# Recurrent LSTM and RNN on one core: ScalarE's bias copy and GpSimd's sums of x are issued at other places

## The chip, the cores and the metric

The kernel runs on one core of one Trainium2 chip. The metric is the device time of one execution in microseconds (us); the number compared is the median of several executions. Times of single instructions come from one further execution, taken with the hardware profiler.

## The reference

Two recurrent layers run one after the other over 512 steps, with 16 sequences side by side and 512 features. Each layer's output is added to its input.

```
# layer 0, an LSTM (xW = x @ Wx + b, h starts at cond_1024, c at 0)
a = xw_t + prev_h @ Wh                      # 16 x 2048
i, f, o = sigmoid(a[:, :H]), sigmoid(a[:, H:2H]), sigmoid(a[:, 2H:3H]);  g = tanh(a[:, 3H:])
next_c = f * prev_c + i * g
next_h = o * tanh(next_c)
x = x + all the next_h
# layer 1, a plain RNN on the new x (h starts at cond_1024)
h_next = tanh(h @ Wh + xw_t)                # 16 x 512
x = x + all the h_next
```

## The kernel before

Everything is transposed: features lie on the 128 partitions, and 512 features are four slices of 128 (`SUB`). TensorE works with four column groups of 32 (`QUADS`), so a "matmul" of the trace is one of four that run beside each other in the array (`128*32` in the rows). The state h is held as an fp16 high part and an fp16 low part, side by side as 32 columns. The recurrent weights of the LSTM are also split in two fp16 tiles.

**One pass of the loop is one step t of the LSTM and, beside it, step s = t - 4 (ScalarE, TensorE) of the RNN.** There is no scheduler: each engine has its own list of instructions, written by hand, in order, and semaphores tie the lists together. In the trace's names, in the order in which TensorE takes them in step t:

- `rec_first_ps` and `rec_second_ps`: 32 matmuls each, the two halves of `prev_h @ Wh`. The first half begins when the low part of the first half of h is ready (`h0_ready[0]`, VectorE line 536), and its second 16 matmuls wait for `h0_ready[1]`, the same line for the second half of h.
- "units", on `in_ps` and `c_ps`: the products x @ Wx of later steps, in fp32. Four steps (a span) need 14 units of 8 matmuls, and they are dealt out as 4, 3, 4, 3 over steps with (t + 5) % 4 = 0, 1, 2, 3. So odd steps have 32 such matmuls and even steps 24. They use sums and differences of blocks of x (`x_sums`), which is how seven products do the work of eight.
- `rnn_ps<-wx_sb,y`: the RNN's x @ Wx for two of its steps at once (`input1`), 24 matmuls in an even step and 8 in an odd one.
- `rnn_ps<-wh_parts,h_parts`: 16 matmuls, the RNN's recurrent product (`recurrent1`).

Before `input1`, TensorE waits for the RNN's seed of this step (`seed1_done`), and in odd steps also for `in1_biased`: ScalarE has then written the bias b1 for the RNN's steps s + 3 and s + 4 into one of two places of `rnn_ps` (`bias1`, line 652). That place has just been read by `seed1(s)` (line 680), which is why the copy can't come before it.

VectorE turns the products (line 483, `turned<-rec_first_ps` and `rec_second_ps`), adds the two parts of h (line 489), forms the cell and then h (lines 509, 514, 524, 529, 536), and writes x + h (line 544, `y<-h_full,x_sb`). In between it handles the RNN: line 550 (`rec_sum<-rnn_ps,rec_low`), the turn at line 556, the add at line 561 (`pre<-turned`), lines 566 and 571 for the RNN's new state. ScalarE writes seeds into PSUM (lines 669, 680) and takes the tanh of the gates (line 693), of the RNN (688) and of the cell (703).

GpSimd, after its setup, does only the sums of x. In each chunk of 16 steps it makes four instructions (line 211, `x_sums`), one per step, for the next chunk, whose units begin at step 11 of the current one. All their operands are in SBUF. The table is `if 3 <= c < 7` at line 235, and each is released by `rec0_done[0]`, the end of the step's `rec_first_ps` matmuls.

Of the kernel before, what the change touches and what calls it, by code (L numbers as in the profile page):

```python
# [19 lines left out]
CHUNKS = STEPS // CHUNK  # L20
# [3 lines left out]
PAIRS = STEPS // PAIR  # L24
SPAN = 2 * PAIR
SPANS, PER_CHUNK = STEPS // SPAN, CHUNK // SPAN
UNITS_OF_PART = (0, 4, 7, 11, 14)
SLOTS = SPAN * SPANS - 5
Y0_PAIRS = 4
LAG = 4  # L30
H_SCALE = 2.0 ** 15
# [8 lines left out]
def residual_lstm_rnn(nc, xT, h0T, wx0, wh0, b0, wx1, wh1, b1, yT):  # L40
    with ExitStack() as ctx:
# [86 lines left out]
        rec0_done, turned0_done, pre0_done = (sem_by_half(n) for n in ("rec0_done", "turned0_done", "pre0_done"))  # L128
        gates_done, uv_done, cell_done = (sem_by_half(n) for n in ("gates_done", "uv_done", "cell_done"))
        o_scaled_done, tanh_c_done = sem_by_half("o_scaled_done"), sem_by_half("tanh_c_done")  # L130
        h0_full_done, h0_ready = sem_by_half("h0_full_done"), sem_by_half("h0_ready")
        y0_done = sem("y0_done")

        in1_biased, in1_done, seed1_done = sem("in1_biased"), sem("in1_done"), sem("seed1_done")
# [52 lines left out]
        @block.gpsimd  # L187
        def _(pool):
            nc.gpsimd.memset(zeros[:, :], 0.0).then_inc(zeroed, 1)
            nc.gpsimd.memset(h_first[:, :, :], 0.0).then_inc(h_zeroed, 1)  # L190
            nc.gpsimd.memset(gates_cell[:, :, GATES], 0.0).then_inc(cell_zeroed, 1)
            nc.gpsimd.iota(partition[:, :], [[0, 1]], 0, 1).then_inc(numbered, 1)
            def reduce_largest(l):
                pool.wait_ge(largest_done, l + 1)
                nc.gpsimd.partition_all_reduce(largest_all[l][:, :], largest[l][:, :], P,
                                               bass.bass_isa.ReduceOp.max).then_inc(reduced, 1)

            def sum_x(v, i):

                x = x_sb[:, v % 2].rearrange("p k (g r t) n -> p r k g (t n)", g=PER_CHUNK, r=2)  # L200
                a11, a12, a21, a22 = x[:, 0, 0:SUBH], x[:, 0, SUBH:SUB], x[:, 1, 0:SUBH], x[:, 1, SUBH:SUB]
                sums = x_sums[:, v % 2]
                if i == 0:
                    pool.wait_ge(x_in[v % 2], loads(v))
                    if v >= 2:
                        pool.wait_ge(slot_done, slots_until((v - 1) * CHUNK - 6))
                if i in (1, 3):
                    pool.wait_ge(x_summed, 4 * v + i)
                out, one, op, other = ((sums[:, 0], a21, ALU.add, a22), (sums[:, 1], sums[:, 0], ALU.subtract, a11),
                                       (sums[:, 2], a11, ALU.subtract, a21), (sums[:, 3], a12, ALU.subtract, sums[:, 1]))[i]  # L210
                nc.gpsimd.tensor_tensor(out, one, other, op).then_inc(x_summed, 1)  # L211

            def sum_wx0(i):

                b11, b12 = wx0_sb[:, 0:SUBH, :, 0:COLSH], wx0_sb[:, 0:SUBH, :, COLSH:COLS]
                b21, b22 = wx0_sb[:, SUBH:SUB, :, 0:COLSH], wx0_sb[:, SUBH:SUB, :, COLSH:COLS]
                if i < 2:
                    pool.wait_ge(wx0_doubled, SUBH * (i + 1))
                if i in (1, 3):
                    pool.wait_ge(wx0_summed, i)  # L220
                one, other = ((b12, b11), (b22, wx0_sums[:, 0]), (b22, b12), (b21, wx0_sums[:, 1]))[i]
                nc.gpsimd.tensor_tensor(wx0_sums[:, i], one, other, ALU.subtract).then_inc(wx0_summed, 1)

            pool.wait_ge(b0_doubled, 1)
            nc.gpsimd.tensor_tensor(b0_diff[:, :], b0_sb[:, COLSH:COLS], b0_sb[:, 0:COLSH], ALU.subtract).then_inc(b0_diff_done, 1)
            for i in range(4):
                sum_x(0, i)
            reduce_largest(0)
            for i in range(4):
                sum_wx0(i)  # L230

            reduce_largest(1)
            for t in range(STEPS):
                v, c = divmod(t, CHUNK)
                if 3 <= c < 7 and v + 1 < CHUNKS:
                    pool.wait_ge(rec0_done[0], t + 1)
                    sum_x(v + 1, c - 3)

        @block.tensor
        def _(pe):  # L240
# [391 lines left out]
        def _(act):  # L632
# [18 lines left out]
            def bias1(r):  # L651
                nc.scalar.activation(in1_ps[r % 2], b1_sb[:, :], ACT.Copy).then_inc(in1_biased, 1)
# [21 lines left out]
            def seed1(s):  # L674

                act.wait_ge(in1_done, s // PAIR + 1)
                if s:
                    act.wait_ge(rec1_summed, s)
                own = (mask_scaled[1] if s else mask_half)[:, s % PAIR:s % PAIR + 1]
                nc.scalar.activation(rec1_by_part, in1_by_part(s // PAIR % 2), ACT.Copy, scale=own).then_inc(seed1_done, 1)  # L680
# [58 lines left out]
            for t in range(END):  # L739
                s = t - LAG  # L740
                g, part = divmod(t + 5, SPAN)
                ahead = t < SLOTS
                if t < STEPS:
                    act.wait_ge(slot_done, slots_until(t - 1))
                    if t:
                        seed0(1, t)
                if s >= 1:
                    copy_low1(s - 1)
                if t < STEPS:
                    if t + 1 < STEPS:  # L750
                        seed0(0, t + 1)
                    if t == 1:
                        copy_v(1)
                    if part == 0 and g < SPANS:
                        act.wait_ge(seed0_done[0], t + 2)
                        bias_z(g).then_inc(z_biased, 1)
                    elif part == 1 and ahead:
                        act.wait_ge(seed0_done[0], t + 2)
                        if g > 1:
                            copy_v(g)  # L760
                        begin_c11(g).then_inc(c11_begun, 1)
                    elif part == 3 and g + 1 < SPANS:
                        bias_v(g + 1).then_inc(v_biased, 1)
                if t == 3:
                    act.wait_ge(scaled, 2)
                    for k in range(SUB):
                        high_part(wh1_sb[:, k].rearrange("p q (b c) -> p (q b) c", c=QUAD), 1,
                                  wh1_parts[:, k, :, :, 0].rearrange("p q b c -> p (q b) c"))
                if 0 <= s < STEPS:
                    seed1(s)  # L770
                if t < STEPS:
                    gates(0, t)
                if s >= 1:
                    tanh1(s - 1)
                if t < STEPS:
                    o_half(0, t)
                    gates(1, t)
                    tanh_cell(0, t)
                if s >= 0 and s % 2 and s // 2 + 2 < PAIRS:

                    act.wait_ge(seed1_done, s + 1)
                    bias1(s // 2 + 2)
                if t < STEPS:
                    o_half(1, t)
                    tanh_cell(1, t)
# [39 lines left out]
```

## Time and profile before

| | us |
|---|---|
| three timed executions, median | 2277.07 |
| lowest and highest | 2273.94 and 2279.57 |
| the profiled execution | 2289.59 |
| its span, first to last instruction | 2287.8 |
| PE busy | 2210.8 (97%) |
| VectorE (DVE) busy | 2100.8 (92%) |
| ScalarE (ACT) busy | 1782.7 (78%) |
| GpSimd (POOL) busy | 116.1 (5%) |

The span lies 1.8 us inside its execution, and that execution is 12.5 us longer than the median of the timed ones. The granted TensorE clock was 0.987 on the mean. The 512 steps fill nearly the whole span, in a steady rhythm: a step takes some 4.3 us. TensorE's matmuls overlap and their ends are modelled, so "busy" does not mean that the array has work all the time; what the engine does between two groups is better seen from the starts of the groups.

### The profile page before, as it was taken

The page shows a single profiled execution, that of the slowest core. Times are in us where ns is not written, and L with a number is a line of the kernel's source. Part 1 is how long each engine was busy: PE and PEld are TensorE (multiplying, and loading weights), DVE is VectorE, ACT ScalarE, POOL GpSimd, SP SyncE. Part 2 cuts the span into 40 slices and gives each one's busy share as a digit, 9 for nine tenths or more (in the row PEclk, how much of TensorE's full clock was granted, in tenths as well). Part 3 has the DMA queues.
Part 4 walks back from the last instruction along what each step waited for, and adds up shares of the span by engine and source line. Part 5 has one row for each costly group of instructions (what it writes and reads, how often), then busy time and mean ns, then how long its engine had stood idle before and what let it go on. Part 6 is the DMA issues. An engine that isn't in the chain of part 4 may idle for free.

```text
span 2287.8 us, 148190 instructions
## 1 busy us (share of the span) xinstructions
PE 2210.8 (97%) x63548; PEld 1835.4 (80%) x63548; DVE 2100.8 (92%) x11050; ACT 1782.7 (78%) x6431; POOL 116.1 (5%) x143
## 2 busy tenths in 40 slices
PE   3899999999999999999999999999999999999996
PEld 1688888888888888888888888888888888888885
DVE  6899999999999999999998999899999999899997
ACT  3688787887887788777887788778887888778885
POOL 4000000000000000000000000000000000000000
PEclk7999999999999999999999999999999999999998
DMA  5000000000000000000000000000000000000000
GB/s 209 3 23 23 18 23 14 18 22 23 18 23 13 18 23 22 18 16 19 18 23 21 19 13 23 18 23 18 23 13 18 23 23 18 22 14 18 23 13 12
DMA packets 16733, 53.88 MB, mean 24 GB/s; under 512 B 2256, under 2 KB 2384, under 8 KB 14800
## 3 DMA queue, kind: packets, MB, share of 16 engines
q1 hardware_dynamic: 16080, 44.41, 5.4%
q8 instruction: 503, 8.24, 1.5%
q14 instruction: 150, 1.23, 0.2%
HBM read 27.62 MB, written 16.78 MB: 19 GB/s over the span
## 4 chain that ended last, share of the span: by engine, by line
PE 95%; DVE 2%; issue 1%; ACT 1%; DMA 1%; POOL 0%; SPq 0%; DVEq 0%; ACTq 0%; POOLq 0%
PE in_ps L244 24%; PE rnn_ps L244 22%; PE rec_first_ps L244 20%; PE rec_second_ps L244 19%; PE c_ps L244 10%; DVE wh_part L452 1%; DMA x_sb<-xT 1%; ACT wh_part L658 0%; DVE turned L483 0%; DVE wh_parts L452 0%; POOL x_sums L211 0%; ACT wh_parts L658 0%; DVE largest_slice L407 0%; ACT gates_cell L693 0%; DVE pre_sb L489 0%
## 5 line engine op out<-in xcount | busy, mean ns | idle before, releaser
L244 PE MATMUL rec_first_ps<-wh_part,h_parts 128*32 128x256 f16 x16352 | 561.2, 273 | 20.7 <-DVE h_parts L536 20.6
L244 PE MATMUL rec_second_ps<-wh_part,h_parts 128*32 128x256 f16 x16352 | 560.9, 273 | 0.1
L244 PEld LDWEIGHTS rec_first_ps<-wh_part,h_parts 128*32 128x32 f16 x16352 | 436.3, 96 | 59.5 <-issue 32.2
L244 PEld LDWEIGHTS rec_second_ps<-wh_part,h_parts 128*32 128x32 f16 x16352 | 469.0, 97 | 1.1 <-issue 0.3
L244 PE MATMUL in_ps<-wx_sums,x_sums 128*32 128x256 f32 x6096 | 417.3, 379 | 2.2 <-issue 1.2
L244 PEld LDWEIGHTS rnn_ps<-wx_sb,y 128*32 128x32 f32 x8192 | 249.7, 109 | 156.4 <-issue 126.8
L693 ACT ACTIVATE gates_cell<-gate_ps,unscale 128x128 f32<-128x128 f32 x511 | 187.9, 368 | 240.3 <-DVE gate_ps L489 237.9
L244 PE MATMUL rnn_ps<-wx_sb,y 128*32 128x128 f32 x8192 | 347.6, 275 | 13.0 <-issue 6.3
L244 PE MATMUL rnn_ps<-wh_parts,h_parts 128*32 128x256 f16 x8176 | 344.8, 274 | 8.2 <-DVE h_parts L571 8.2
L244 PEld LDWEIGHTS in_ps<-wx_sums,x_sums 128*32 128x32 f32 x6096 | 225.2, 110 | 92.7 <-issue 4.7
L244 PEld LDWEIGHTS rnn_ps<-wh_parts,h_parts 128*32 128x32 f16 x8176 | 249.9, 97 | 11.4 <-issue 8.5
L483 DVE STREAM_TRANSPOSE turned<-rec_second_ps 128x256 f32<-128x256 f32 x512 | 228.9, 447 | 18.8 <-PE rec_second_ps L244 0.9
L550 DVE TENSOR_TENSOR rec_sum<-rnn_ps,rec_low 128x128 f32<-128x128 f32 x512 | 149.5, 292 | 94.7 <-ACT rec_low L684 88.6
L680 ACT ACTIVATE rnn_ps<-rnn_ps,mask_scaled 128x256 f32<-128x256 f32 x511 | 225.4, 441 | 12.7 <-DVE rec_sum L550 2.5
L693 ACT ACTIVATE gates_cell<-pre_sb,unscale 128x128 f32<-128x128 f32 x511 | 205.4, 402 | 30.6 <-DVE pre_sb L489 1.3
L509 DVE SCALAR_TENSOR_TENSOR uv<-gates_cell 128x64 f32<-128x64 f32 x1024 | 227.2, 222 | 1.8 <-ACT gates_cell L693 1.4
L684 ACT ACTIVATE rec_low<-rnn_ps 128x128 f32<-128x128 f32 x512 | 142.1, 278 | 107.9 <-PE rnn_ps L244 96.1
L483 DVE STREAM_TRANSPOSE turned<-rec_first_ps 128x256 f32<-128x256 f32 x512 | 219.9, 430 | 2.5 <-PE rec_first_ps L244 1.1
L698 ACT ACTIVATE o_scaled<-gates_cell 128x32 f32<-128x32 f32 x1024 | 219.8, 215 | 0.2
L536 DVE TENSOR_TENSOR h_parts<-h_full,h_parts 128x32 f16<-128x32 f32 x1024 | 193.0, 188 | 17.9
L244 PE MATMUL c_ps<-wx_sb,x_sb 128*32 128x256 f32 x2096 | 174.6, 383 | 24.1 <-ACT wx_sb L634 24.0
L514 DVE SCALAR_TENSOR_TENSOR gates_cell<-uv 128x32 f32<-128x32 f32 x1024 | 193.6, 189 | 0.2
(93 smaller groups left out, 3575.8 us busy)
## 6 DMA issues: line engine op xcount, KB each, us to landing
x_sb<-xT SPq DMA_DIRECT2D x32, 512.0 KB, 4.1
yT<-y SPq DMA_DIRECT2D x64, 256.0 KB, 2.4
wh_sb<-wh SPq DMA_DIRECT2D x5, 1024.0 KB, 9.0
wx_sb<-wx SPq DMA_DIRECT2D x5, 1024.0 KB, 14.4
b_sb<-b SPq DMA_DIRECT2D x1, 256.0 KB, 2.7
b_sb<-b SPq DMA_DIRECT2D x1, 64.0 KB, 11.6
h_first<-h0T SPq DMA_DIRECT2D x1, 32.0 KB, 11.3
```

Source lines behind the costliest of these rows:

```text
L244: last = nc.tensor.matmul(out[QUAD * q:QUAD * (q + 1)], states, weights(q), start=False, stop=True, tile_position=(0, QUAD * q), skip_grou ...
L452: return nc.vector.scalar_tensor_tensor(low, w32, w_scale[l][:, :], high, ALU.mult, ALU.subtract)
L483: nc.vector.transpose(turned0[:, half].rearrange("p b n -> p (b n)"), rec0_ps(t, half)).then_inc(turned0_done[half], 1)
L509: nc.vector.scalar_tensor_tensor(uv[:, half], gates_cell[:, half, 0:2], 1.0, gates_cell[:, half, 3:5], ALU.add, ALU.mult).then_inc(uv_done ...
L514: nc.vector.scalar_tensor_tensor(gates_cell[:, half, GATES], uv[:, half, 1], 0.5, uv[:, half, 0], ALU.mult, ALU.add).then_inc(cell_done[ha ...
L536: nc.vector.tensor_tensor(h0_parts[:, subs, BATCH:], slices(h0_full[:, cols]), h0_parts[:, subs, 0:BATCH], ALU.subtract).then_inc(h0_ready ...
L550: nc.vector.tensor_tensor(rec1_sum[:, :, :], rec1_by_part[:, :, 0], rec1_low[:, :, :], ALU.add).then_inc(rec1_summed, 1)
L680: nc.scalar.activation(rec1_by_part, in1_by_part(s // PAIR % 2), ACT.Copy, scale=own).then_inc(seed1_done, 1)
L684: nc.scalar.activation(rec1_low[:, :, :], rec1_by_part[:, :, 1], ACT.Copy).then_inc(rec1_copied, 1)
L693: nc.scalar.activation(gates_cell[:, half, 0:GATES].rearrange("p g n -> p (g n)"), pre0[half], ACT.Tanh, scale=unscale[0][:, :] if t else ...
L698: nc.scalar.activation(o_scaled[:, half], gates_cell[:, half, 2], ACT.Copy, bias=H_SCALE / 2, scale=H_SCALE / 2).then_inc(o_scaled_done[ha ...
```

## The change

Two moves; no instruction is added or removed.

1. ScalarE: `bias1` of odd RNN steps is issued straight behind `seed1`, ahead of the tanh of the first half's gates. Before it stood behind `tanh_cell(0, t)`. It still waits for `seed1_done`.
2. GpSimd: the four sums of a chunk are made in steps 3, 4, 7 and 8 instead of 3, 4, 5 and 6, and each waits for `h0_ready[1]` to reach t (the state that step t starts from is complete) instead of `rec0_done[0]` reaching t + 1 (step t's first product is done).

```diff
+STEPS_OF_X_SUMS = (3, 4, 7, 8)
...
             for t in range(STEPS):
                 v, c = divmod(t, CHUNK)
-                if 3 <= c < 7 and v + 1 < CHUNKS:
-                    pool.wait_ge(rec0_done[0], t + 1)
-                    sum_x(v + 1, c - 3)
+                if c in STEPS_OF_X_SUMS and v + 1 < CHUNKS:
+                    pool.wait_ge(h0_ready[1], t)
+                    sum_x(v + 1, STEPS_OF_X_SUMS.index(c))
...
                 if 0 <= s < STEPS:
                     seed1(s)
+                if s >= 0 and s % 2 and s // 2 + 2 < PAIRS:
+
+                    act.wait_ge(seed1_done, s + 1)
+                    bias1(s // 2 + 2)
                 if t < STEPS:
                     gates(0, t)
                 if s >= 1:
...
                     gates(1, t)
                     tanh_cell(0, t)
-                if s >= 0 and s % 2 and s // 2 + 2 < PAIRS:
-
-                    act.wait_ge(seed1_done, s + 1)
-                    bias1(s // 2 + 2)
                 if t < STEPS:
                     o_half(1, t)
                     tanh_cell(1, t)
```

ScalarE's list in an odd step (t = 7), before, from the second half's seed to the last tanh. `rnn_ps<-b_sb` is the bias copy, `rnn_ps<-rnn_ps,mask_scaled` the RNN's seed:

```order
L669 ACTIVATE rec_second_ps<-c_sb,mask_scaled 128x256 [waits turned0_done_1,slot_done]
L684 ACTIVATE rec_low<-rnn_ps 128x128 [waits rec1_done]
L669 ACTIVATE rec_first_ps<-c_ps,mask_scaled 128x256 [waits turned0_done_0]
L637 ACTIVATE in_ps<-b_sb 128x256 [waits seed0_done_0]
L680 ACTIVATE rnn_ps<-rnn_ps,mask_scaled 128x256 [waits rec1_summed,in1_done]
L693 ACTIVATE gates_cell<-gate_ps,unscale 128x128 [waits pre0_done_0]
L688 ACTIVATE h_full<-pre,unscale 128x64 [waits pre1_done]
L698 ACTIVATE o_scaled<-gates_cell 128x32 [waits gates_done_0]
L693 ACTIVATE gates_cell<-pre_sb,unscale 128x128 [waits pre0_done_1]
L703 ACTIVATE gate_ps<-gates_cell 128x32 [waits cell_done_0]
L652 ACTIVATE rnn_ps<-b_sb 128x128 [waits seed1_done]
L698 ACTIVATE o_scaled<-gates_cell 128x32 [waits gates_done_1]
```

The same place in the changed kernel, whose lines are numbered one higher:

```order
L670 ACTIVATE rec_second_ps<-c_sb,mask_scaled 128x256 [waits turned0_done_1,slot_done]
L685 ACTIVATE rec_low<-rnn_ps 128x128 [waits rec1_done]
L670 ACTIVATE rec_first_ps<-c_ps,mask_scaled 128x256 [waits turned0_done_0]
L638 ACTIVATE in_ps<-b_sb 128x256 [waits seed0_done_0]
L681 ACTIVATE rnn_ps<-rnn_ps,mask_scaled 128x256 [waits rec1_summed,in1_done]
L653 ACTIVATE rnn_ps<-b_sb 128x128 [waits seed1_done]
L694 ACTIVATE gates_cell<-gate_ps,unscale 128x128 [waits pre0_done_0]
L689 ACTIVATE h_full<-pre,unscale 128x64 [waits pre1_done]
L699 ACTIVATE o_scaled<-gates_cell 128x32 [waits gates_done_0]
L694 ACTIVATE gates_cell<-pre_sb,unscale 128x128 [waits pre0_done_1]
L704 ACTIVATE gate_ps<-gates_cell 128x32 [waits cell_done_0]
L699 ACTIVATE o_scaled<-gates_cell 128x32 [waits gates_done_1]
```

The bias copy moved five places forward: it now stands in front of the tanh of the first gates, directly behind the instruction whose semaphore it waits for.

GpSimd's list of the first sums in the loop, before (the four of chunk 1 and the first of chunk 2):

```order
L211 TENSOR_TENSOR x_sums<-x_sb 128x256 [waits x_in1,rec0_done_0]
L211 TENSOR_TENSOR x_sums<-x_sums,x_sb 128x256 [waits x_summed,rec0_done_0]
L211 TENSOR_TENSOR x_sums<-x_sb 128x256 [waits rec0_done_0]
L211 TENSOR_TENSOR x_sums<-x_sb,x_sums 128x256 [waits x_summed,rec0_done_0]
L211 TENSOR_TENSOR x_sums<-x_sb 128x256 [waits slot_done,x_in0,rec0_done_0]
```

And in the changed kernel:

```order
L212 TENSOR_TENSOR x_sums<-x_sb 128x256 [waits x_in1,h0_ready_1]
L212 TENSOR_TENSOR x_sums<-x_sums,x_sb 128x256 [waits x_summed,h0_ready_1]
L212 TENSOR_TENSOR x_sums<-x_sb 128x256 [waits h0_ready_1]
L212 TENSOR_TENSOR x_sums<-x_sb,x_sums 128x256 [waits x_summed,h0_ready_1]
L212 TENSOR_TENSOR x_sums<-x_sb 128x256 [waits slot_done,x_in0,h0_ready_1]
```

Their order is the same; what releases each of them is another semaphore (and, for the third and fourth, a later step).

## Rows read from the trace of the kernel before

**Rows 1.** The page: busy us of each engine, share of the span, count.

```profile
PE 2210.8 (97%) x63548; PEld 1835.4 (80%) x63548; DVE 2100.8 (92%) x11050; ACT 1782.7 (78%) x6431; POOL 116.1 (5%) x143
```

**Rows 2.** Waits: engine, releaser, us in total, times, longest us.

```profile
PEld rnn_ps L244 <- issue: 135.3, 277, 2.7
...
PE rec_first_ps L244 <- DVE h_parts L536: 20.6, 7, 16.0
```

**Rows 3.** Timeline of odd step 203: start us, length us, engine, operation, count.

```profile
937.24 1.05 PE L244 MATMUL in_ps<-wx_sb,x_sb 128*32 128x256 f32 x16
...
938.78 0.26 ACT L652 ACTIVATE rnn_ps<-b_sb 128x128 f32<-128x128 f32 x1
...
939.11 0.19 PEld L244 LDWEIGHTS rnn_ps<-wx_sb,y 128*32 128x32 f32 x8 [0.44 <-issue]
...
939.14 0.43 PE L244 MATMUL rnn_ps<-wx_sb,y 128*32 128x128 f32 x8
...
939.30 0.19 DVE L536 TENSOR_TENSOR h_parts<-h_full,h_parts 128x32 f16<-128x32 f32 x1
...
939.36 0.65 PE L244 MATMUL rnn_ps<-wh_parts,h_parts 128*32 128x256 f16 x16
...
939.80 1.08 PE L244 MATMUL rec_first_ps<-wh_part,h_parts 128*32 128x256 f16 x32
```

**Rows 4.** Timeline of even step 204, matmuls (PE), weight loads (PEld), VectorE.

```profile
941.54 1.07 PE L244 MATMUL in_ps<-wx_sums,x_sums 128*32 128x256 f32 x16
...
942.84 0.87 PE L244 MATMUL rnn_ps<-wx_sb,y 128*32 128x128 f32 x24
...
943.62 0.19 DVE L536 TENSOR_TENSOR h_parts<-h_full,h_parts 128x32 f16<-128x32 f32 x1
...
943.93 0.81 PEld L244 LDWEIGHTS rec_first_ps<-wh_part,h_parts 128*32 128x32 f16 x32
...
943.96 1.06 PE L244 MATMUL rec_first_ps<-wh_part,h_parts 128*32 128x256 f16 x32
```

**Rows 5.** Timeline of ScalarE in odd step 203.

```profile
936.69 0.43 ACT L680 ACTIVATE rnn_ps<-rnn_ps,mask_scaled 128x256 f32<-128x256 f32 x1
...
937.42 0.37 ACT L693 ACTIVATE gates_cell<-gate_ps,unscale 128x128 f32<-128x128 f32 x1 [0.30 <-DVE gate_ps L489]
...
938.28 0.40 ACT L693 ACTIVATE gates_cell<-pre_sb,unscale 128x128 f32<-128x128 f32 x1
```

**Rows 6.** Timeline around one sum of x (POOL) and VectorE beside it.

```profile
1050.08 0.30 DVE L556 STREAM_TRANSPOSE turned<-rec_sum 128x128 f32<-128x128 f32 x1
1050.27 0.73 POOL L211 TENSOR_TENSOR x_sums<-x_sb 128x256 f32<-128x256 f32 x1 [3.51 <-PE rec_first_ps L244]
1050.31 0.41 DVE L483 STREAM_TRANSPOSE turned<-rec_first_ps 128x256 f32<-128x256 f32 x1
1050.64 0.44 DVE L561 TENSOR_TENSOR pre<-turned 128x64 f32<-128x64 f32 x1
```

**Rows 7.** Line 561: length ns min/median/max, first and last start.

```profile
L561 DVE TENSOR_TENSOR pre<-turned x512: 179/184/492, 85.9 to 2284.1; 128x64 f32<-128x64 f32 x171
```

**Rows 8.** Line 211, in the same columns.

```profile
L211 POOL TENSOR_TENSOR x_sums<-x_sums,x_sb x32: 729/733/1247, 15.8 to 2151.3; 128x256 f32<-128x256 f32 x32
```

**Rows 9.** Stretches of four steps: length, busy us (count) by engine, clock, DMA.

```profile
902.35:919.67 17.32, 17.15 (x506) 14.07 (x497) 16.48 (x88) 13.69 (x52) 2.93 (x4) 1.00 0.06 19
936.60:953.53 16.93, 16.93 (x505) 14.07 (x497) 15.88 (x87) 13.80 (x51) 0.00 (x0) 1.00 0.06 20
```

**Rows 10.** Timeline of VectorE from the end of step 203 into step 204.

```profile
939.81 0.18 DVE L536 TENSOR_TENSOR h_parts<-h_full,h_parts 128x32 f16<-128x32 f32 x1
...
939.91 0.22 DVE L544 SCALAR_TENSOR_TENSOR y<-h_full,x_sb 128x64 f32<-128x64 f32 x1
...
940.36 0.29 DVE L550 TENSOR_TENSOR rec_sum<-rnn_ps,rec_low 128x128 f32<-128x128 f32 x1 [0.23 <-ACT rec_low L684]
...
941.29 0.18 DVE L561 TENSOR_TENSOR pre<-turned 128x64 f32<-128x64 f32 x1
```

## The prediction

> **What bounds the kernel now.** I read the page's first part, then the view of waits, then two steps instruction by instruction, then GpSimd's four instructions of a chunk.
>
> The page has TensorE busy for 97% of the span, VectorE for 92% [rows 1]. That could mean a kernel bound by matmuls, where nothing that ScalarE or GpSimd does can matter. The view of waits says otherwise: TensorE's weight loads for the RNN stood still 277 times, 135.3 us in all, 0.49 us each [rows 2]. The releaser is given as "issue", so the profile doesn't name it. But 277 is little more than 254, the number of odd RNN steps with a bias copy (s = 1, 3, ..., 507), and the timeline shows it. In odd step 203 the units begin at 937.24, the bias copy runs from 938.78 to 939.04, and the weight loads of `input1` begin at 939.11 after 0.44 us of idle time, 0.07 us behind the copy's end; the first matmul is at 939.14 [rows 3]. So TensorE waits for the copy in every odd step.
>
> Those 0.44 us are not what the wait costs, because loads run ahead of matmuls. The cost is read from the starts of the matmuls. In even step 204, 24 fp32 matmuls of the units lie between 941.54 and 942.84: 1.30 us, 0.054 us each [rows 4]. Thirty-two take 1.73 us, so in step 203 `input1` could begin at 937.24 + 1.73 = 938.97 and not at 939.14. The wait costs 0.17 us of a step.
>
> The second bound is the state. In step 204 the first half's low part ends at 943.62 + 0.19 = 943.81, the weight loads of the next `rec_first_ps` begin 0.12 us later, at 943.93, and its matmuls at 943.96 [rows 4]. That is a wait for the state, which only just binds: from the end of line 536 to the first matmul there are 0.15 us. In step 203 the same part ends at 939.49, and the matmuls begin at 939.80, 0.31 us later [rows 3]: there the state is early and TensorE late. From one `rec_first_ps` to the next, step 204 takes 943.96 - 939.80 = 4.16 us, with the state as its limit.
>
> **Part one, the bias copy.** Nothing is added, one copy of 0.26 us moves. On ScalarE the RNN's seed ends at 937.12 and the tanh of the first gates begins at 937.42, when VectorE has its input [rows 5]. The copy waits for the seed's own semaphore, for which I take 0.03 us: 937.15 to 937.41. It fits into the hole of 0.30 us with 0.01 us to spare. If it is late by some hundredths, the tanh of the first gates is late by as much; that tanh has no hurry, because ScalarE's next one that matters starts at 938.28 for an input of its own. In its old place the copy ran while VectorE formed the second cell, so its leaving speeds up nothing on ScalarE.
>
> TensorE then finds the copy done 1.5 us before it asks. `input1` starts at 938.97. The RNN's product starts 0.22 us later (939.36 - 939.14) and the next `rec_first_ps` 0.44 us after that (939.80 - 939.36) [rows 3]: 939.63. What is late next is the state: 939.49 + 0.15 = 939.64. The two limits nearly meet, and the gain is 939.80 - 939.64 = 0.16 us. I take 0.15, as one step's difference is read to 0.01 and the other kind of odd step may have less. 254 x 0.15 = 38.1 us. Bounds: TensorE can't gain more than the 0.17 of the wait, 43 us; it gains nothing if the state, once pulled, comes no earlier. The state should follow, since everything between two states starts from TensorE's products. I take off 2 us for odd steps in which TensorE's stalls of other kinds are now hidden in the wait (23 of the 277 are such, if all 254 are the copy's): 36 us.
>
> **Part two, the sums.** A sum takes 0.73 us on GpSimd, and it is always followed by the same thing. The one at 1050.27 ends at 1051.00. VectorE's add of line 561, with both inputs in SBUF, begins at 1050.64 and takes 0.44 us; it ends at 1051.08, 0.08 us behind the sum. The transpose before it (one input, in PSUM) ran from 1050.31 for 0.41 us, inside the sum, and the transpose at 1050.08 (one input, in SBUF) overlaps it as well; neither kept the other up [rows 6]. Line 561 has a median of 184 ns and a maximum of 492 [rows 7], so the sums hold it up by up to 0.3 us. It also goes the other way: one sum took 1247 ns where 733 is the median [rows 8], at 79.2 us, among VectorE's long two-input instructions of the setup. One waits for the whole of the other.
>
> The Trainium skill ("SBUF — State Buffer", § Who interferes with whom) states that a VectorE instruction with two SBUF inputs and a GpSimd instruction that reads SBUF share one port pair, that whichever starts first keeps it for its whole length, and that VectorE with at most one SBUF input doesn't contend. The rows agree so far.
>
> The price comes from two stretches that begin and end at the same place of the rhythm: four steps with four sums take 17.32 us, four without any 16.93 [rows 9]. So a chunk's sums cost 0.39 us, and 31 chunks 12.1 us.
>
> Where do they fall in the changed kernel? The state is complete at 939.81 + 0.18 = 939.99. The y add of line 544 is then already running, 939.91 to 940.13, and has two SBUF inputs. Line 550 at 940.36 has one input in PSUM, and line 561 comes at 941.29 [rows 10], some 0.16 us earlier in the new rhythm: 941.13. A sum released at 939.99 runs from about 940.03, or from 940.13 if it has to let the y add finish, and ends at 940.76 to 940.86. Nothing with two SBUF inputs is due until 941.13. The sums become free: 12 us are saved. The same stretch ahead of the other kind of chosen step is shorter but, by the same count, holds a sum too. The fourth sum is ready in step 8 and needed in step 11, so no unit is late, and no queue stands behind GpSimd's wait, as it has no other work.
>
> **The sum.** 36 + 12 = 48 us, from the profiled execution's 2289.6 to 2241.6 (span 2287.8 to 2240). The timed median is 12.5 us below the profiled execution; taking the same 48 from it gives 2229. I say 2230.
>
> **Rivals.**
>
> A. *The state doesn't follow.* The new limit of an odd step lies 0.01 us from TensorE's own, and every chain through ScalarE and VectorE is close. If an odd step gains 0.05 instead of 0.15, part one brings 12.7 us, and the whole 25: 2252. For it speaks that VectorE is busy for 92%; against it that the state of step 203 waits 0.16 us unused today.
>
> B. *The sum overtakes the y add.* The sum is released at 939.99, 0.08 us after the add's row begins [rows 10]. If the add doesn't hold the port by then, it waits for the sum, as line 561 does, and ends at 940.03 + 0.73 + 0.08 = 940.84. Line 550 is queued behind it and would start near 940.8, not at 940.36 - 0.16 = 940.20: 0.6 us late. Part of that is slack: the second turn waits for `rec_second_ps` anyway, and I put this slack at 0.2 us. 0.4 x 124 sums = 50 us, which eats all 48: 2279, no change. The 1247 ns sum speaks against it, for there the instruction that was running went first.
>
> C. *The same mechanism at full price*, with no slack in the turn: 0.6 x 124 = 74 us against 48, slower by 26 us: 2303. It ends on the slower side once a sum costs over (48 + 7) / 124 = 0.44 us. The place is the two-input add ahead of line 550, and the price is the 0.6 above.
>
> By the Trainium skill's rule of who starts first (same page and section) the y add, whose row begins 0.08 us ahead of the release, keeps the port, and B and C don't happen; no row shows two such instructions that close.
>
> D. *The bias copy isn't what TensorE waits for* but `seed1_done` or y. Then only the sums' 12 us remain: 2265. The 0.07 us between the copy's end and the loads speaks against it.
>
> **How the numbers follow.** The forecast has 0.68, A 0.14, B 0.06, C 0.04, D 0.04, and 0.04 goes to something not seen, spread evenly over both signs. A measurement of this kernel can't tell less than about 0.3% (7 us) from no change. A and D are faster by more than that. Faster: 0.68 + 0.14 + 0.04 + 0.02 = 0.88. Same: B with a bit of the rest, 0.07. Slower: 0.05. The range begins where the whole wait of 0.17 is won and 0.39 per chunk too (55 us: 2222), with 4 us for what a single profile misses, and reaches past A: 2218 to 2256.
>
> **What the new profile would show.** The 277 waits of the weight loads for `rnn_ps` fall to some tens. In an odd step the matmuls of `input1` begin 1.73 us behind the first of the units, and `rec_first_ps` 0.15 us behind the end of line 536 in every step, odd or even. The bias copy sits between the RNN's seed and the first gates' tanh, which hardly moves. Line 561 has no length above 0.2 us in the loop, and line 544 stays at 0.22; B and C would show it at 0.8 or more. Sums have 0.73 to 0.85 us. Four steps take 16.93 - 2 x 0.15 = 16.63 us with sums and without. The prediction is wrong if the four steps stay near 16.9, or if those with sums are longer than those without.

## The result: 2214.9 us, 2.8% faster, and more than predicted

The changed kernel takes 2214.85 us in the median of four executions (2212.09 to 2216.77), the kernel before 2278.32 beside it. The ratio is 0.9724, with a 95% interval of 0.9706 to 0.9741: faster by 63 us, where 48 were predicted. The time lies 3 us below the low end of the range (2218). The direction and both mechanisms held; the size was too small.

The profiled execution is one of the four, 2214.99 us, with a span of 2213.2. Its first part answers to [rows 1]:

```profile
PE 2146.7 (97%) x63548; PEld 1769.1 (80%) x63548; DVE 2092.3 (95%) x11050; ACT 1808.4 (82%) x6431; POOL 116.5 (5%) x143
```

The same 97% of TensorE, in a kernel that is 3% shorter: this share says nothing about the wait that went. The view of waits (engine, what was waited for, us in total, times, longest) does, where [rows 2] had 135.3 us in 277 waits for `rnn_ps`:

```profile
PEld rec_first_ps L245 <- issue: 25.6, 21, 16.5
PE rec_first_ps L245 <- DVE h_parts L537: 20.6, 8, 16.0
...
PEld rnn_ps L245 <- issue: 8.0, 3, 2.7
```

Three waits are left of 277. In the timeline of odd step 203, which answers to [rows 3] and [rows 5] (start and length in us):

```profile
911.04 0.43 ACT L681 ACTIVATE rnn_ps<-rnn_ps,mask_scaled 128x256 f32<-128x256 f32 x1
...
911.50 0.28 ACT L653 ACTIVATE rnn_ps<-b_sb 128x128 f32<-128x128 f32 x1
911.59 1.05 PE L245 MATMUL in_ps<-wx_sb,x_sb 128*32 128x256 f32 x16
911.77 0.37 ACT L694 ACTIVATE gates_cell<-gate_ps,unscale 128x128 f32<-128x128 f32 x1
...
913.32 0.41 PE L245 MATMUL rnn_ps<-wx_sb,y 128*32 128x128 f32 x8
...
913.65 0.19 DVE L537 TENSOR_TENSOR h_parts<-h_full,h_parts 128x32 f16<-128x32 f32 x1
...
913.99 1.06 PE L245 MATMUL rec_first_ps<-wh_part,h_parts 128*32 128x256 f16 x32
```

The copy follows its seed, and the first gates' tanh still begins 0.73 us behind that seed's start (937.42 - 936.69 before, 911.77 - 911.04 now). The RNN's input product begins 913.32 - 911.59 = 1.73 us behind the units, as computed. The next `rec_first_ps` begins 0.15 us behind the end of line 537 (913.65 + 0.19 = 913.84): the state's limit. Even step 204 answers to [rows 4]:

```profile
917.80 0.19 DVE L537 TENSOR_TENSOR h_parts<-h_full,h_parts 128x32 f16<-128x32 f32 x1
918.11 0.81 PEld L245 LDWEIGHTS rec_first_ps<-wh_part,h_parts 128*32 128x32 f16 x32
918.14 1.06 PE L245 MATMUL rec_first_ps<-wh_part,h_parts 128*32 128x256 f16 x32
```

From 913.99 to 918.14 are 4.15 us, with 0.15 us behind line 537 again. It is so throughout: in 99% of the steps from 30 to 490 of this trace that distance is 0.15 us, where the kernel before has it at the end of undisturbed even steps alone (42% of all steps; 0.30 us in a typical odd one). The state is now the limit of odd and even steps alike.

A sum of x and VectorE beside it, from the timeline at step 200:

```profile
897.58 0.18 DVE L537 TENSOR_TENSOR h_parts<-h_full,h_parts 128x32 f16<-128x32 f32 x1
897.68 0.22 DVE L545 SCALAR_TENSOR_TENSOR y<-h_full,x_sb 128x64 f32<-128x64 f32 x1
897.84 0.73 POOL L212 TENSOR_TENSOR x_sums<-x_sb,x_sums 128x256 f32<-128x256 f32 x1 [3.42 <-DVE h_parts L537]
897.92 0.29 DVE L551 TENSOR_TENSOR rec_sum<-rnn_ps,rec_low 128x128 f32<-128x128 f32 x1
...
898.88 0.18 DVE L562 TENSOR_TENSOR pre<-turned 128x64 f32<-128x64 f32 x1
```

The sum starts 0.08 us behind the complete state and ends at 898.57. The y add keeps its 0.22 us, line 551 its 0.29 beside the sum, and line 562, the add that used to wait, starts 0.31 us after the sum's end. Over the whole kernel (length in ns: min/median/max) line 562 answers to [rows 7], whose maximum was 492; the y add of line 545, beside which each of the 120 sums of the 480 steps from 16 to 496 starts, never took more than 222:

```profile
L562 DVE TENSOR_TENSOR pre<-turned x512: 182/183/226, 87.4 to 2209.5; 128x64 f32<-128x64 f32 x171
L545 DVE SCALAR_TENSOR_TENSOR y<-h_full,x_sb x512: 216/219/222, 64.0 to 2195.1; 128x64 f32<-128x64 f32 x171
```

### The profile page after: what moved, and what is told of

Same layout as the page of the kernel before. It is cut to its first block, busy times and chain, and to the rows that moved or that the text cites. A ratio compares the mean times of both kernels' runs of the same rounds, so it can differ in the third digit from the quotient of the medians.

```text
span 2213.2 us, 148190 instructions
## 1 busy us (share of the span) xinstructions
PE 2146.7 (97%) x63548; PEld 1769.1 (80%) x63548; DVE 2092.3 (95%) x11050; ACT 1808.4 (82%) x6431; POOL 116.5 (5%) x143
## 4 chain that ended last, share of the span: by engine, by line
PE 95%; DVE 2%; issue 1%; ACT 1%; DMA 1%; POOL 0%; SPq 0%; DVEq 0%; ACTq 0%; POOLq 0%
PE in_ps L245 25%; PE rec_first_ps L245 21%; PE rec_second_ps L245 20%; PE rnn_ps L245 20%; PE c_ps L245 10%; DVE wh_part L453 1%; DMA x_sb<-xT 1%; ACT wh_part L659 0%; DVE turned L484 0%; DVE wh_parts L453 0%; POOL x_sums L212 0%; DVE uv L510 0%; ACT wh_parts L659 0%; DVE largest_slice L408 0%; DVE pre_sb L490 0%
## 5 line engine op out<-in xcount | busy, mean ns | idle before, releaser
L245 PE MATMUL rec_first_ps<-wh_part,h_parts 128*32 128x256 f16 x16352 | 545.4, 274 | 20.9 <-DVE h_parts L537 20.6
L245 PE MATMUL rec_second_ps<-wh_part,h_parts 128*32 128x256 f16 x16352 | 544.5, 273 | 0.0
L245 PEld LDWEIGHTS rec_first_ps<-wh_part,h_parts 128*32 128x32 f16 x16352 | 377.8, 95 | 105.9 <-issue 25.3
L245 PEld LDWEIGHTS rec_second_ps<-wh_part,h_parts 128*32 128x32 f16 x16352 | 454.3, 97 | 0.4
L245 PE MATMUL in_ps<-wx_sums,x_sums 128*32 128x256 f32 x6096 | 402.1, 379 | 1.4 <-ACT rec_first_ps L670 0.7
L245 PE MATMUL rnn_ps<-wh_parts,h_parts 128*32 128x256 f16 x8176 | 322.0, 273 | 11.7 <-DVE h_parts L572 11.7
L245 PE MATMUL rnn_ps<-wx_sb,y 128*32 128x128 f32 x8192 | 321.9, 273 | 1.5 <-ACT rnn_ps L681 1.5
L245 PEld LDWEIGHTS in_ps<-wx_sums,x_sums 128*32 128x32 f32 x6096 | 206.0, 110 | 102.2 <-issue 2.1
L245 PEld LDWEIGHTS rnn_ps<-wh_parts,h_parts 128*32 128x32 f16 x8176 | 230.6, 97 | 14.6 <-issue 8.0
L704 ACT ACTIVATE tanh_c_sb<-gates_cell 128x32 f32<-128x32 f32 x512 | 118.0, 231 | 108.5 <-DVE gates_cell L515 108.5
```

The source lines that it names most:

```text
L245: last = nc.tensor.matmul(out[QUAD * q:QUAD * (q + 1)], states, weights(q), start=False, stop=True, tile_position=(0, QUAD * q), skip_grou ...
L704: nc.scalar.activation(tanh_c[half], gates_cell[:, half, GATES], ACT.Tanh, scale=0.5).then_inc(tanh_c_done[half], 1)
```

## The experiments

All are timed against the kernel before, on the same chip in the same job; its medians there were 2278.7 to 2282.4. The changed kernel's 2214.9 comes from a job of its own (2278.3 before), so differences of some 4 us from it are within what the jobs differ by. Two numbers are read from each profile. Steps 16 to 496 are cut into 30 chunks of 16 steps, each from the start of one step's turn of `rec_first_ps` (line 484 in the changed kernel, 483 in the one before) to that of the step 16 later. The **regular time** is the shortest of these chunks, which holds four sums like every other. The **irregular time** is what the 480 steps take beyond 30 times the regular time.

### Each part alone

The copy moved, the sums as before:

```diff
-                if c in STEPS_OF_X_SUMS and v + 1 < CHUNKS:
-                    pool.wait_ge(h0_ready[1], t)
-                    sum_x(v + 1, STEPS_OF_X_SUMS.index(c))
+                if 3 <= c < 7 and v + 1 < CHUNKS:
+                    pool.wait_ge(rec0_done[0], t + 1)
+                    sum_x(v + 1, c - 3)
```

> The bias copy moved as in the change; the sums of x as in the kernel before. Theory 1 (two separate parts: the copy's place is worth 0.165 us in each of 254 odd steps, 42 us, and with it most of TensorE's irregular stalls go, some 9 us): 51 us below before, 2227. Theory 2 (the stalls go with the sums, not with the copy): 42 us below, 2236. Theory 3 (the sums' contention costs more once the state bounds every step, since all of it lands on the state): less than 40 us, 2240 or more.

Measured: 2223.39 us, ratio 0.9749 (0.9725 to 0.9772), 56 us below before.

The sums moved, the copy as before (the change's second part alone):

```diff
-                if 3 <= c < 7 and v + 1 < CHUNKS:
-                    pool.wait_ge(rec0_done[0], t + 1)
+                if c in STEPS_OF_X_SUMS and v + 1 < CHUNKS:
+                    pool.wait_ge(h0_ready[1], t)
```

> The sums of x as in the changed kernel; the bias copy in its old place. Theory 1: 12 us below before, 2266, and the stalls are still there. Theory 2: 12 + 9 = 21 us below, 2257. Theory 3: under 12 us.

Measured: 2265.04 us, ratio 0.9933 (0.9909 to 0.9956), 14.5 us below before. With the changed kernel at 2214.9, the sums' move is worth 8.5 us when the copy has been moved. Theory 1 comes closest, with 51 and 12 us expected for the two parts alone and 56 and 14.5 measured. Theory 2 (42 us and 21) and theory 3 fall.

### Does anything remain?

The changed kernel with sums for two chunks only:

```diff
-                if c in STEPS_OF_X_SUMS and v + 1 < CHUNKS:
+                if c in STEPS_OF_X_SUMS and v + 1 < 2:
...
-                pe.wait_ge(x_summed, 4 * (g // PER_CHUNK) + i + 1)
+                pe.wait_ge(x_summed, min(4 * (g // PER_CHUNK) + i + 1, 8))
```

> The changed kernel with the sums of x made only for the first two chunks; all later chunks use those. If the sums are free in their new place, as the prediction says, the time is the changed kernel's, 2215 within 3 us. If they still hold something up, it is lower by what they cost.

Measured: 2212.17 us. Its regular time is 66.32 us against 66.37: by that, 120 sums together cost under 2 us; by the timed medians the kernel is 2.7 us faster. The sums are as good as free.

The kernel before without the loop's bias copies and TensorE's waits for them:

```diff
-                if s >= 0 and s % 2 and s // 2 + 2 < PAIRS:
-
-                    act.wait_ge(seed1_done, s + 1)
-                    bias1(s // 2 + 2)
...
-                    if s % 2 and s // 2 + 2 < PAIRS:
-                        pe.wait_ge(in1_biased, s // 2 + 3)
...
-                pe.wait_ge(in1_biased, r + 1)
+                pe.wait_ge(in1_biased, min(r + 1, 2))
```

> The kernel before without the bias copies of the loop and without TensorE's waits for them (the RNN's input sums then pile up on old ones); the sums of x as before. If the wait for the copy is all that its old place costs, this is as fast as the kernel with only the copy moved, 2227 by theory 1. If the copy in its new place still costs something (it delays the first gates' tanh), this one is faster than that kernel.

Measured: 2223.98 us, the same as with the copy moved (2223.39). In its new place the copy costs nothing.

### What bounds the changed kernel

Less work for TensorE in odd steps:

```diff
                     j, k = divmod(u, 2)
+                    if g > 1 and u in (3, 9):
+                        continue
```

> The changed kernel with two of the 14 units of a span left out, the second halves of the product with the first sum and of that with the third sum (one in each odd step, 8 fp32 matmuls, 0.43 us; the LSTM's input is wrong). If the state bounds the odd steps now, as I worked out (TensorE's own limit lies 0.02 us below), the time stays at 2215, at most 5 us less. If TensorE's work bounds them, it falls by up to 0.43 x 254 = 109 us.

Measured: 2211.36 us, as expected if the state is the limit: 109 us of matmuls went, and the time fell by 3.5 us at most. The waits of the weight loads show where the rest is, now ahead of `rec_first_ps`, where the changed kernel had 25.6 us in 21:

```profile
PEld rec_first_ps L245 <- issue: 141.4, 267, 17.2
```

So the state bounds the steps, and TensorE's work doesn't.

A try at shortening the state's path, VectorE's products of the first half ahead of the add of the second:

```diff
                     turn0(1, t)
-                    add0(1, n)
                     gate_products(0, n)
+                    add0(1, n)
```

> The changed kernel with VectorE's gate products of the first half ahead of the add of the second half. If the state's first half bounds every step, its cell is formed up to 0.05 us earlier, and TensorE's own limit of 4.12 to 4.13 us a step against 4.15 allows 0.02 us a step, 10 us: 2205. If the second half, which comes 0.02 to 0.04 us later, bounds as well, nothing is gained or some 10 us lost.

Measured: 2233.35 us, ratio 0.9785 (0.9771 to 0.9800), slower than the changed kernel by 18.5 us, beyond what either guess allowed. Its regular time says the same: (66.96 - 66.37) / 16 = 0.037 us a step. The timeline of VectorE in this kernel, in a step of the kind (t + 5) % 4 = 2:

```profile
927.13 0.45 DVE L484 STREAM_TRANSPOSE turned<-rec_second_ps 128x256 f32<-128x256 f32 x1
927.62 0.23 DVE L510 SCALAR_TENSOR_TENSOR uv<-gates_cell 128x64 f32<-128x64 f32 x1
927.76 0.28 DVE L490 TENSOR_TENSOR pre_sb<-turned 128x128 f32<-128x128 f32 x1
```

And in the changed kernel:

```profile
903.53 0.45 DVE L484 STREAM_TRANSPOSE turned<-rec_second_ps 128x256 f32<-128x256 f32 x1
904.01 0.29 DVE L490 TENSOR_TENSOR pre_sb<-turned 128x128 f32<-128x128 f32 x1
904.22 0.22 DVE L510 SCALAR_TENSOR_TENSOR uv<-gates_cell 128x64 f32<-128x64 f32 x1
```

The second half's add comes 0.63 us behind the turn's start and not 0.48: the product stands in front of it in the list. So the second half of the state has too little slack to be put back by that much, and moving work from the first half onto it loses.

### What about the sums matters: the steps, or the place within the step?

The changed steps with the old release:

```diff
-                    pool.wait_ge(h0_ready[1], t)
+                    pool.wait_ge(rec0_done[0], t + 1)
```

> The changed kernel, its sums in steps 3, 4, 7 and 8 but released by the end of the step's first product as before. Theory P (what matters is when in the step the sum runs, since VectorE's two-input add of line 562 waits for it): as slow as the kernel with only the copy moved, 2223, with line 562 at up to 0.49 us. Theory S (what matters is which steps): 2215.

Measured: 2225.15 us. The old steps with the changed release:

```diff
-STEPS_OF_X_SUMS = (3, 4, 7, 8)
+STEPS_OF_X_SUMS = (3, 4, 5, 6)
```

> The changed kernel with the sums in steps 3, 4, 5 and 6, released by the complete state as in the change. Theory P (only the place within the step matters): as fast as the changed kernel, 2215, line 562 never above 0.23 us. Theory S (steps 5 and 6 are worse, since VectorE also has the adds of lines 498 and 505 there): between 2215 and 2223.

Measured: 2214.44 us, the changed kernel's time. Line 562 in the one and in the other:

```profile
L562 DVE TENSOR_TENSOR pre<-turned x512: 180/183/492, 86.9 to 2219.5; 128x64 f32<-128x64 f32 x171
```

```profile
L562 DVE TENSOR_TENSOR pre<-turned x512: 179/182/226, 88.2 to 2209.8; 128x64 f32<-128x64 f32 x171
```

All of the sums' gain comes from the release: with it the kernel is as fast as the changed one, without it as slow as with the copy moved alone (2223.39). No run shows a gain from the new table of steps.

### The stalls outside the rhythm

A made-up wait of TensorE in odd steps, with the copy in its new place:

```diff
                         pe.wait_ge(in1_biased, s // 2 + 3)
+                        pe.wait_ge(o_scaled_done[1], t + 1)
```

> The changed kernel, in which TensorE waits in every odd step, ahead of the RNN's input product, for ScalarE's scaled o gate of the second half as well. That instruction ends about where the bias copy ended in its old place, so the made-up wait takes about the time of the old one, with the copy in its new place. Theory W (the irregular stalls come with TensorE's wait in the odd steps, whatever it waits for): some 40 us slower than the changed kernel by rhythm and 10 to 20 by stalls, 2255 to 2275, and the stalls are back in the trace. Theory C (they come from the copy's place on ScalarE): 40 us slower at most, with 4 to 5 us of irregular time as now, 2250 to 2255.

Measured: 2283.5 us, ratio 1.0011 (0.9999 to 1.0023): the whole gain is gone, more than either theory expected. In an odd step the loads behind the made-up wait begin 0.06 us later than those behind the old one (0.50 us of idle time against 0.44), so the rhythm cost more than expected, and the irregular time is back.

A made-up wait in even steps:

```diff
+                if 8 <= t < STEPS and t % 2 == 0:
+                    pe.wait_ge(gates_done[1], t + 1)
                 if 2 <= t < STEPS:
```

> The changed kernel, in which TensorE waits in even steps, ahead of the RNN's input product, for the tanh of the second half's gates, some 0.2 us. By rhythm 0.18 x 252 = 45 us slower than the changed kernel, 2260. If a wait in the middle of the step brings stalls wherever it stands, 10 to 20 us more, 2270 to 2280, with irregular time of 10 to 25 us; if only the odd steps' place does, 4 to 5 us of irregular time.

Measured: 2293.75 us, ratio 1.0052 (1.0033 to 1.0070), slower still and above the 2270 to 2280 expected; its rhythm, too, costs more than expected (68.37 us for 16 steps). The irregular time, 19.4 us, is what was expected if a wait brings it wherever it stands.

The kernel before once more, for its profile:

> The kernel before, for a second profile. Question: how much of the irregular time in its first profile (25 us beyond the regular rhythm of steps 16 to 500) is a property of the kernel. By theory W (TensorE's wait in odd steps brings the stalls) 10 to 25 us again; if the first profile was a chance, under 6 us, as in all kernels without that wait.

Measured, in a single execution: 2279.02 us, with 16 us of irregular time, where under 6 was expected if the first profile had been a chance.

Without the loads of x after the second chunk, then also without the stores of y after the second group, in the kernel before and in the changed one:

```diff
-                    sp.dma_start(x_sb[:, (v + 1) % 2], xT[v + 1]).then_inc(x_in[(v + 1) % 2], 16)
...
-                if s % GROUP == GROUP - 1:
+                if s % GROUP == GROUP - 1 and s < 2 * GROUP:
```

> The kernel before without the loads of x from the third chunk on (the first two chunks are used again and again); all waits in TensorE's list stay. If the stalls come from TensorE's instructions arriving late behind the 512 KB loads, they go, and the time falls by the 10 to 15 us of irregular time, to 2265. If the loads have no part in it, 2278 and 10 to 25 us of irregular time.

Measured: 2276.23 us, ratio 0.9976 (0.9964 to 0.9988): 3 us less, and not the 10 to 15 expected if the loads were the cause.

> The kernel before without the loads of x from the third chunk on and without the stores of y after the first two groups; TensorE's list and its wait for the bias copy stay. Theory D (the irregular stalls are TensorE's instructions that arrive late behind data transfers, and a wait in the middle of a step makes it prone to that): irregular time falls from 16 to 26 us to about 5, the time to 2265. Theory N (the data transfers have no more part in it than the 8 us that the missing loads showed): irregular time stays at 8 or more, 2272 to 2276.

Measured: 2272.4 us, ratio 0.9972 (0.9961 to 0.9983), 6 us less: theory N.

> The changed kernel, with the same transfers left out. Theory D: the 5 us of irregular time shrink too, by 0 to 5 us: 2210 to 2215. Theory N: 2215, with 5 us of irregular time.

Measured: 2210.95 us, with the regular and irregular time of the changed kernel. Of the 4 us, 3 lie behind step 496, where the last stores are gone.

All profiles side by side:

| kernel | TensorE waits in mid-step | regular, 16 steps | irregular in 480 steps |
|---|---|---|---|
| before, first and second profile | odd | 68.11, 68.10 | 26.3, 16.1 |
| sums moved alone | odd | 67.69 | 12.4 |
| before without loads | odd | 68.11 | 8.4 |
| before without loads and stores | odd | 68.10 | 11.8 |
| made-up wait, odd steps | odd | 68.20 | 17.3 |
| made-up wait, even steps | even | 68.37 | 19.4 |
| changed | no | 66.37 | 5.3 |
| copy moved alone | no | 66.70 | 4.3 |
| no bias copy | no | 66.69 | 4.8 |
| changed without sums | no | 66.32 | 5.5 |
| fewer units | no | 66.33 | 3.5 |
| products first | no | 66.96 | 5.2 |
| new steps, old release | no | 66.73 | 5.3 |
| old steps, new release | no | 66.35 | 6.7 |
| changed without loads and stores | no | 66.35 | 5.1 |

The rows behind it are those of the view of stretches (length, then busy us by engine): first the 480 steps, then the 16. The kernel before in its second profile:

```profile
133.65:2192.75 2059.10, 2049.96 (x59530) 1705.06 (x59523) 1925.45 (x10322) 1649.86 (x6001) 87.84 (x120) 1.00 0.06 20
201.78:269.88 68.10, 67.93 (x1993) 56.27 (x1985) 64.17 (x345) 54.95 (x201) 2.92 (x4) 1.00 0.06 20
```

The changed kernel:

```profile
133.20:2129.59 1996.39, 1996.09 (x59529) 1653.53 (x59521) 1916.68 (x10321) 1676.61 (x6001) 88.06 (x120) 1.00 0.06 20
133.20:199.57 66.37, 66.37 (x1993) 54.53 (x1985) 63.79 (x345) 55.86 (x201) 2.94 (x4) 1.00 0.06 20
```

And the made-up wait in odd steps:

```profile
133.71:2197.02 2063.31, 2047.28 (x59529) 1706.85 (x59522) 1907.16 (x10321) 1674.96 (x6001) 88.02 (x120) 1.00 0.06 20
1855.13:1923.33 68.20, 67.78 (x1993) 56.27 (x1986) 63.52 (x345) 55.88 (x201) 2.94 (x4) 1.00 0.06 20
```

Before: 2059.10 - 30 x 68.10 = 16.1. Changed: 1996.39 - 30 x 66.37 = 5.3. TensorE shows no matmul for 9.1 us of the before kernel's 480 steps, of which 30 x 0.17 = 5.1 belong to its rhythm; for 0.3 us of the changed kernel's; and for 16.0 us, of which 30 x 0.42 = 12.6 belong to the rhythm, with the made-up wait. So idle time of the matmuls shows only 3 to 4 us of an irregular time of 16 to 17. The rest is seen in the starts of the groups and in the loads. What such a stall looks like, among the weight loads of the kernel before (first profile):

```profile
964.55 0.19 PEld L244 LDWEIGHTS rnn_ps<-wx_sb,y 128*32 128x32 f32 x8 [0.37 <-issue]
...
968.24 0.37 PEld L244 LDWEIGHTS in_ps<-wx_sums,x_sb 128*32 128x32 f32 x11 [0.71 <-issue]
...
977.13 0.11 PEld L244 LDWEIGHTS in_ps<-wx_sums,x_sums 128*32 128x32 f32 x1 [0.20 <-issue]
```

The first gap is the wait for the copy. The others stand in the middle of a group of 16 loads, where the list has no wait. They come in trains that set in near steps 42, 108, 154, 210, 266, 322, 386 and 433 in this profile; the changed kernel has short ones near 63, 119, 178, 234, 291, 347, 406 and 462. So they recur about every 56 or 57 steps in both, and grow into trains only where TensorE waits in mid-step.

That period can be compared with another one in the same traces, that of the packets which bring instructions. In the kernel before and in the one with fewer units, the pages have (packets, MB, share of the DMA engines' time):

```profile
q8 instruction: 503, 8.24, 1.5%
```

```profile
q8 instruction: 487, 7.98, 1.5%
```

With 2016 matmuls and 2016 weight loads fewer there are 16 packets of 16 KB fewer, so this queue carries TensorE's instructions, about 250 in a packet. A step has nearly as many. Fitted over the 480 steps, a packet starts every 1.0179 steps in the changed kernel, so that its place within the step comes round every 1.0179 / 0.0179 = 57.0 steps. Where a kernel changes the one period, the other follows ("long" is a step that takes over 0.08 us more than the median of those at its place in the chunk):

| kernel | a packet every | its place comes round every | the main runs of long steps begin near |
|---|---|---|---|
| changed | 1.0179 steps | 57.0 steps | 63, 119, 178, 234, 291, 347, 406, 462 |
| made-up wait, even steps | 1.0159 | 64.1 | 41, 105, 169, 233, 297, 361, 429 |
| no bias copy | 1.0200 | 51.1 | 58, 110, 208, 263, 313, 361, 418, and some halfway |
| fewer units | 1.0514 | 20.5 | 66, 86, 167, 230, 250, 313, 333, 353, 394, 475, 495 |

And of the 302 gaps of over 0.15 us that the 16 profiles have inside groups of weight loads, none begins in the first 1.1 us behind the start of a packet, though packets start only some 4.3 us apart; of the 93 in the nine kernels without the wait none begins in the first 1.8 us. So when a stall comes is tied to the supply of TensorE's instructions.

## Why the prediction was wrong in size

**What bounds the kernel: right.** TensorE waited for the bias copy in every odd step, and the state was the next limit. The trace of the changed kernel shows each step of the argument (1.73 us, 0.15 us, the gates' tanh in its place), and leaving the copy out altogether gains no more. Predicted were 36 + 12 = 48 us; 63 came. Some 5 of the missing 15 us lie in the regular time, the rest in the stalls.

**The bias copy, regular part: 38 us predicted for the whole kernel, which is 36 for 480 steps; 41 measured in those.** Four steps without sums took 16.93 us [rows 9]. In the changed kernel, in the same view:

```profile
910.95:927.54 16.59, 16.59 (x505) 13.63 (x497) 15.94 (x87) 13.96 (x51) 0.00 (x0) 1.00 0.06 20
```

That is 0.34 us for four steps and 120 x 0.34 = 41 us in 480 steps, where the prediction had 0.30. A chunk with its four sums now takes 66.37 us, and 4 x 16.59 is 66.36: the four steps are as long with sums as without, as the prediction asked. The odd steps gained what was said: from one `rec_first_ps` to the next, in steps without sums, their median went from 4.300 to 4.149 us. The rest came from the even steps, which I took as already bound by the state: 4.167 to 4.151.

**The stalls: 2 us taken off, 8 to 11 gained.** This is the step that failed: "I take off 2 us for odd steps in which TensorE's stalls of other kinds are now hidden in the wait". The sign was wrong. The stalls are not a fixed cost beside the wait; they come with it. The two profiles at the timed level differ by 2059.10 - 1996.39 = 62.7 us in 480 steps: 30 x (68.10 - 66.37) = 51.9 regular and 16.1 - 5.3 = 10.8 irregular. Stretched to 512 steps the regular part is 55.4 us, which leaves 8 of the 63.5 between the timed medians. With a made-up wait, in odd or in even steps, the stalls were there; without one, in nine kernels, they were small. Each number is from one profile, and two profiles of the same kernel differed by 10 us, but the two groups don't overlap. I had looked at typical steps only. The trace itself would have shown the excess: 30 x 68.1 us is 26 us short of what 480 steps took in the profile that I read.

**The sums: 12.1 us predicted, 8.5 to 14.5 measured.** In regular time 68.10 - 67.69 = 0.41 us a chunk with the copy in its old place and 66.70 - 66.37 = 0.33 with it in the new one, 10 to 13 us for 31 chunks. The mechanism is as stated, and the y add was not overtaken.

**The baseline.** I subtracted from the median, not from the profiled execution. That was right: the profile read was 12.5 us long, and the second one, at 2279.0 us, has the same regular time and 10 us less of stalls.

**The range** reached to 55 us of gain, the sum of both bounds for the regular parts, and 4 us for what a single profile misses. It had no room for a stall that depends on the wait. Of the rivals, A (the state doesn't follow) is refuted by the 0.15 us behind line 537 in 99% of the steps, B and C by the y add, at most 222 ns in 512 steps, D by the 56 us of the copy moved alone.

**Open.** Why the stalls grow when TensorE waits in mid-step isn't settled. Data transfers have a part at most: without them the irregular time was 8 and 12 us instead of 16 to 26, still above the 6.7 us that is the most of any kernel without the wait, and in the changed kernel their absence made no difference to it (5.1 against 5.3 us). The stalls come in step with the packets of TensorE's instructions, in every kernel. That tells when they come. How a wait in mid-step makes them longer isn't shown, and no run varied the supply while the wait stayed as it was.

## What to carry to other kernels

When an engine list is in order, ask of every small instruction when its result is first needed and when its input is free; put it in the earliest hole after its input, and count the cost from the starts of the waiting engine's work, not from its idle time (0.44 us of idle loads here, 0.17 us of matmuls). Set the sum of typical steps against the whole stretch before predicting: what is left over may belong to the thing that is about to be changed. An instruction that makes another engine wait belongs where that engine runs operations that don't wait for it; here the release within the step decided, and the choice of steps nothing.

## What the runs showed of the hardware

- A GpSimd instruction that reads SBUF kept a VectorE add with two SBUF inputs waiting until 0.08 us behind its own end (492 ns instead of 184), and left VectorE's instructions with one SBUF input alone, the transposes and also line 551 (one input in PSUM: 0.29 us inside each of 120 sums, a case that the trace of before doesn't have). This is the rule of the Trainium skill ("SBUF — State Buffer", § Who interferes with whom). When a y add had been under way for 0.16 us as a sum began, so that their rows overlap by some 0.06 us, neither was longer, in 120 such pairs: the adds took at most 222 ns, the sums at most 740.
- TensorE's weight loads stood still for 0.44 us where its matmuls lost 0.17. The Trainium skill ("TensorE: Matmul & The Clock Gate", § Architectural detail: the array is 16× 32×32, not 1× 128×128) says that TensorE's queue can pull weight loads ahead of matmuls in flight; the trace agrees, and such a gap overstates the loss.
- Unexpected: TensorE's loads stood still for 0.2 to 1.1 us outside any wait of its list. The steps that this made longer cost 3.5 to 6.7 us in 480 steps in nine kernels without a mid-step wait and 8 to 26 us in the seven profiles of kernels with one. They recur as the packets of TensorE's instructions come round within the step: every 57, 64, 51 or 20.5 steps, as the kernel has it.
